# Turning the weights ahead of the codes, and 24 of 128 one-hot columns on ScalarE, in a product-key expert stage

## The reference

```
x_norm = x * rsqrt(mean(x * x) + eps) * norm_w
q = (x_norm @ wq).reshape(B, T, HEADS, 2, DIM_KEY)              # 8 heads, 2 halves, 32
sim = einsum('bthpd,hkpd->pbthk', q, keys)                      # 64 keys for each half
s1, i1 = top_k(sim[0], 16);  s2, i2 = top_k(sim[1], 16)
all_idx = (i1[..., :, None] * 64 + i2[..., None, :]).reshape(B, T, HEADS, 256)
all_scores = (s1[..., :, None] + s2[..., None, :]).reshape(B, T, HEADS, 256)
final_scores, pk = top_k(all_scores, 16)
final_idx = take_along_axis(all_idx, pk)
hidden = einsum('btd,bthkd->bthk', x_norm, expert_down[final_idx])
hidden = gelu(hidden) * relu(final_scores)
out = einsum('bthk,bthkd->btd', hidden, expert_up[final_idx])
```

## Time and profile before

| | us |
|---|---|
| median of 3 runs | 2354.24 |
| the runs | 2340.14 to 2354.62 |
| the profiled execution | 2347.7 |
| its span, first to last instruction | 2346.0 |
| first and last start of L2000 (expert stage's one-hots) | 648.1 and 1781.7 |

### The profile page before, as it was taken

The page is one execution under the profiler, slowest core; times in us unless marked ns, Lnnn a source line. Parts: engine busy times, 40 slices in busy tenths (PEclk is TensorE's granted clock), DMA queues, the critical chain, the costliest instruction groups (busy, mean ns, idle before and its releaser), DMA issues. The chain is left out here.

```text
span 2346.0 us, 48081 instructions
## 1 busy us (share of the span) xinstructions
PE 1891.4 (81%) x17539; PEld 1539.1 (66%) x17539; DVE 1628.3 (69%) x6887; ACT 732.5 (31%) x1593; POOL 558.1 (24%) x779
## 2 busy tenths in 40 slices
PE   6595899996178978889789789897889699737995
PEld 3364688874167867778677677786778577634653
DVE  3433566654999999999999999999993577420112
ACT  1343255554132231322313223132131255422220
POOL 2002344431021403304124042140431310031111
PEclk8697899998589989989899898898989799858997
DMA  2232444423500000000000000000000333212424
GB/s 61 67 103 58 103 107 102 106 49 89 131 2 6 6 2 5 2 6 6 2 6 6 2 6 2 6 6 2 2 2 1 73 83 84 87 50 78 149 99 124
DMA packets 90418, 110.21 MB, mean 47 GB/s; under 512 B 27168, under 2 KB 79088, under 8 KB 89552
## 3 DMA queue, kind: packets, MB, share of 16 engines
q1 hardware_dynamic: 84672, 99.09, 16.1%
q0 software_dynamic: 3344, 6.53, 0.8%
q10 hardware_dynamic: 2176, 1.61, 0.2%
HBM read 69.84 MB, written 33.83 MB: 44 GB/s over the span
## 5 line engine op out<-in xcount | busy, mean ns | idle before, releaser
L1568 POOL TENSOR_TENSOR peer_g<-peer_g,peer_qt 128x512 f32<-128x512 f32 (+1 forms) x208 | 250.1, 1213 | 871.1 <-ACT peer_qt L1775 871.1
L1662 PE MATMUL peer_out_ps<-peer_g,peer_up 128*128 128x256 f32 (+1 forms) x1664 | 375.5, 389 | 0.0
L1630 PE MATMUL peer_x_ps<-peer_xc,peer_dt 128*128 128x256 f32 (+1 forms) x1664 | 359.9, 379 | 0.0
L1662 PEld LDWEIGHTS peer_out_ps<-peer_g,peer_up 128*128 128x128 f32 x1664 | 324.3, 202 | 46.6
L1630 PEld LDWEIGHTS peer_x_ps<-peer_xc,peer_dt 128*128 128x128 f32 x1664 | 313.3, 195 | 42.0
L1284 DVE TENSOR_REDUCE l_attn_mx<-l_attn_s_ps 98x4 f32<-98x392 f32 (+1 forms) x320 | 174.7, 559 | 142.2 <-PE l_attn_s_ps L1054 102.5
L1652 PE MATMUL peer_x_ps<-peer_oh_h,peer_oh_a 128*128 128x32 bf16 x3136 | 167.8, 180 | 86.3 <-DVE peer_oh_l L2004 85.7
L1652 PEld LDWEIGHTS peer_x_ps<-peer_oh_h,peer_oh_a 128*128 128x128 bf16 x3136 | 163.1, 99 | 102.2 <-issue 59.0
L2000 DVE TENSOR_TENSOR peer_oh_a<-peer_a_t,peer_iota_f 128x8192 bf16<-128x8192 bf16 x49 | 216.5, 4419 | 1.3
L1775 ACT ACTIVATE peer_qt<-peer_x_ps 128x512 f32<-128x512 f32 (+1 forms) x208 | 119.1, 573 | 239.3 <-PE peer_x_ps L1630 223.5
L1205 ACT ACTIVATE l_attn_pt<-l_attn_st_ps 98x392 f32<-98x392 f32 x320 | 148.3, 492 | 142.4 <-PE l_attn_st_ps L1067 141.3
(11 more groups left out here) (325 smaller groups left out, 3536.7 us busy)
## 6 DMA issues: line engine op xcount, KB each, us to landing
moe_w<-in_L_ffn_w_dram SPq DMA_DIRECT2D x16, 1024.0 KB, 7.8
l_attn_pieces_q_dram<-l_attn_pieces_q SPq DMA_DIRECT2D x16, 294.0 KB, 3.9
l_attn_pieces_k_dram<-l_attn_pieces_k SPq DMA_DIRECT2D x16, 294.0 KB, 3.1
l_attn_stq<-l_attn_pieces_q_dram SPq DMA_DIRECT2D x16, 294.0 KB
l_attn_stk<-l_attn_pieces_k_dram SPq DMA_DIRECT2D x16, 294.0 KB
peer_g<-n_L_ffn_expert_down_dram SPq DMA_DIRECT2D x8, 512.0 KB
peer_up<-in_L_ffn_expert_up_dram SPq DMA_DIRECT2D x2, 2048.0 KB, 17.8
moe_expert_in<-l_blank SPq DMA_DIRECT2D x16, 197.5 KB
```

The source lines that it names most:

```text
L1568: nc.gpsimd.tensor_tensor(pair, pair, act_out[jp % 2][:, :, 0:cols], ALU.mult).then_inc(g_done, 1)
L1630: mm = nc.tensor.matmul(x_ps[b][:, jj * CT:jj * CT + cols], dt[:, k, 2 * jp + jj, :], xc[p][:, k, 0:cols], start=(k == 0), stop=(k == KC - 1))
L1662: mm = nc.tensor.matmul(out_ps[:, m * CT:m * CT + cols], up[:, j, m * P:(m + 1) * P], g[:, j, 0:cols], start=(j == 0), stop=(j == J - 1))
```

## The change

Five things change, all in `peer_ffn`.

The weights no longer go with the codes. When the second top-16 is through, VectorE sets a semaphore (`found`); ScalarE clamps the weights and splits off the high part (`split_weights`), GpSimd subtracts for the low part (`low_parts`), TensorE turns both after the first half of `experts_out` (`turn_weights`), and ScalarE copies them to `wh_t` and `wl_t` (`weights_out`). `low_weights` on VectorE goes.

The column code is made before the row code, and each has its own signal. TensorE turns the columns of both tiles into `tr_ps` and then the rows of both into `sim_ps[1]`; ScalarE copies them in the order b, a, b, a.

VectorE's row one-hots cover columns 0 to 103. ScalarE makes columns 104 to 127 (`side_columns`): for each of the 24 columns it writes the absolute difference of `a_t` and the column's number, 64 tokens, and then one pass over all 24 writes relu(1 - difference).

The column one-hots (`oh_l`) now come first in `one_hots`, and `add_out` stands behind the third block in place of the first.

`side_columns` for blocks 0 and 1 stands at the head of ScalarE's chunk; for block hb + 2 it stands behind the copies of block hb.

The core of the diff:

```diff
-        codes = behind(1, 3 * PP, 3 * PP, F32).rearrange("t (s k) -> t s k", s=3)
+        codes = behind(1, 3 * PP, 2 * PP, F32).rearrange("t (s k) -> t s k", s=2)
+        w_all, w_high, w_low = (behind(1, (5 + i) * PP, PP, F32) for i in range(3))
+        w_rounded = behind(1, 7 * PP, PP // 2, BF16)
...
-        TURN_AT = J // 2
+        WEIGHTS_AT, TURN_AT = (0, J - 1), (1, J // 2 - 1)
...
+            nc.gpsimd.iota(col_bias[:, 0:ACOLS], [[-1, ACOLS]], base=ACOLS - P, channel_multiplier=0,
+                           allow_small_or_imprecise_dtypes=True).then_inc(iota_done, 1)
+            nc.gpsimd.memset(col_bias[:, ACOLS:ACOLS + 1], 1.0).then_inc(iota_done, 1)
...
+            def low_parts(n):
+
+                pool.wait_ge(w_split, n + 1)
+                nc.gpsimd.tensor_tensor(w_low, w_all, w_high, ALU.subtract).then_inc(low_made, 1)
...
                     index_steps(n + 1)
+                    low_parts(n + 1)
...
-            def turn(n, t, rows):
-                pe.wait_ge(codes_ready, n + 1)
-                wait(pe, tr_ready, NTILE * n + t)
-                wait(pe, wl_ready, NTILE * n + t)
-                for s in range(3):
-                    mm = nc.tensor.transpose(tr_ps[:, s * TT:s * TT + rows], codes[0:rows, s, t * NP:(t + 1) * NP], ident[0:rows, 0:rows])
-                mm.then_inc(tr_done, 1)
+            def turn_weights(n, tiles):
+                pe.wait_ge(low_made, n + 1)
+                pe.wait_ge(sim_ready, NTILE * n + len(tiles))
+                for s, source in enumerate((w_high, w_low)):
+                    for t, rows in enumerate(tiles):
+                        mm = nc.tensor.transpose(sim_ps[0][:, (s * NTILE + t) * TT:(s * NTILE + t) * TT + rows],
+                                                 source[0:rows, t * NP:(t + 1) * NP], ident[0:rows, 0:rows])
+                mm.then_inc(w_tr_done, 1)
+
+            def turn(n, tiles):
+                wait(pe, b_ready, NTILE * n)
+                wait(pe, sim_ready, NTILE * n + len(tiles))
+                for s, bank in ((1, tr_ps), (0, sim_ps[1])):
+                    pe.wait_ge(codes_ready, 2 * n + 2 - s)
+                    for t, rows in enumerate(tiles):
+                        nc.tensor.transpose(bank[:, t * TT:t * TT + rows], codes[0:rows, s, t * NP:(t + 1) * NP],
+                                            ident[0:rows, 0:rows]).then_inc(tr_done, 1)
...
                 pe.wait_ge(oh_ready, NHB * n + hb + 1)
+                pe.wait_ge(side_ready, NHB * n + hb + 1)
...
-                        if m == KC - 1 and j == TURN_AT:
-                            for t, rows in enumerate(next_rows):
-                                turn(n + 1, t, rows)
-                mm.then_inc(out_done, 1)
+                        if m == KC - 1 and j == J - 1:
+                            mm.then_inc(out_done, 1)
+                        if (m, j) == WEIGHTS_AT and next_rows:
+                            turn_weights(n + 1, next_rows)
+                        if (m, j) == TURN_AT and next_rows:
+                            turn(n + 1, next_rows)
...
-            def turned(n, t, rows):
-                act.wait_ge(tr_done, NTILE * n + t + 1)
-                ts = slice(t * TT, t * TT + rows)
-                if t == 0:
-                    wait(act, oh_ready, NHB * n)
-                for dst, c in ((wh_t, 2), (a_t, 0), (b_t, 1)):
-                    ins = nc.scalar.activation(dst[:, ts, :], tr_ps[:, c * TT:c * TT + rows].unsqueeze(2).broadcast_to([P, rows, R]), ACT.Copy)
-                ins.then_inc(tr_ready, 1)
-
-            for t in range(NTILE):
-                turned(0, t, TT)
+            def side_columns(n, hb):
+                q = hb % 2
+                wait(act, m_done, 16 * n + 4 * (hb - 1))
+                act.wait_ge(a_ready, NTILE * n + hb // 2 + 1)
+                ts = slice(hb * HT, (hb + 1) * HT)
+                for k in range(ACOLS):
+                    ins = nc.scalar.activation(oh_a[q][:, :, P - ACOLS + k], a_t[:, ts, 0], ACT.Abs, bias=col_bias[:, k:k + 1])
+                ins.then_inc(abs_done, 1)
+                act.wait_ge(abs_done, NHB * n + hb + 1)
+                side = oh_a[q][:, :, P - ACOLS:P]
+                nc.scalar.activation(side, side, ACT.Relu, scale=-1.0, bias=col_bias[:, ACOLS:ACOLS + 1]).then_inc(side_ready, 1)
+
+            def split_weights(n):
+                act.wait_ge(found, n + 1)
+                fv = f16.rearrange("t h k -> t (h k)")
+                nc.scalar.activation(w_rounded, fv, ACT.Relu).then_inc(rounded, 1)
+                nc.scalar.activation(w_all, fv, ACT.Relu)
+                act.wait_ge(rounded, n + 1)
+                nc.scalar.activation(w_high, w_rounded, ACT.Copy).then_inc(w_split, 1)
+
+            def weights_out(n, cols):
+                act.wait_ge(w_tr_done, n + 1)
+                wait(act, oh_ready, NHB * n)
+                for s, dst in enumerate((wh_t, wl_t)):
+                    ins = nc.scalar.activation(dst[:, 0:cols, :], sim_ps[0][:, s * CT:s * CT + cols].unsqueeze(2).broadcast_to([P, cols, R]), ACT.Copy)
+                ins.then_inc(w_ready, 1)
+
+            def turned(n, tiles):
+                for t, rows in enumerate(tiles):
+                    ts = slice(t * TT, t * TT + rows)
+                    for i, (dst, bank, ready) in enumerate(((b_t, tr_ps, b_ready), (a_t, sim_ps[1], a_ready))):
+                        act.wait_ge(tr_done, 2 * NTILE * n + (i + 1) * len(tiles))
+                        nc.scalar.activation(dst[:, ts, :], bank[:, t * TT:t * TT + rows].unsqueeze(2).broadcast_to([P, rows, R]),
+                                             ACT.Copy).then_inc(ready, 1)
+
+            split_weights(0)
+            weights_out(0, CT)
+            turned(0, [TT] * NTILE)
 
             def chunk(n, p, now, then):
                 next_rows = tile_rows(then)
+                n_hb = now // HT
+                for hb in range(min(2, n_hb)):
+                    side_columns(n, hb)
                 wait(act, out_done, n)
-                for hb in range(now // HT):
+                for hb in range(n_hb):
                     scattered(n, hb)
                     if hb == 0 and then > 0:
                         wait(act, g_done, NPAIR * n)
                         query_out(n + 1, then)
                     if 0 < hb <= len(next_rows):
                         score_out(n + 1, hb - 1, next_rows[hb - 1])
+                    if hb + 2 < n_hb:
+                        side_columns(n, hb + 2)
                 hidden_out(n, now)
-                for t, rows in enumerate(next_rows):
-                    turned(n + 1, t, rows)
+                if then > 0:
+                    split_weights(n + 1)
+                    weights_out(n + 1, then)
+                turned(n + 1, next_rows)
...
-                chain.step(nc.vector.tensor_scalar(codes[:, 2, :], fv, 0.0, None, ALU.max))
+                nc.vector.memset(pad[:, 7:8], 0.0).then_inc(found, 1)
+                wait(dve, tr_done, 2 * NTILE * n)
...
-                nc.vector.tensor_tensor(row, by_rank(t1), by_rank(i1), ALU.add)
                 nc.vector.scalar_tensor_tensor(column, by_rank(t1), -0.5, by_rank(i2), ALU.mult, ALU.add).then_inc(codes_ready, 1)
-
-            def low_weights(n, t, rows):
-                dve.wait_ge(tr_ready, NTILE * n + t + 1)
-                ts = slice(t * TT, t * TT + rows)
-                nc.vector.tensor_tensor(wl_t[:, ts, :], tr_ps[:, 2 * TT:2 * TT + rows].unsqueeze(2).broadcast_to([P, rows, R]),
-                                        wh_t[:, ts, :], ALU.subtract).then_inc(wl_ready, 1)
+                nc.vector.tensor_tensor(row, by_rank(t1), by_rank(i1), ALU.add).then_inc(codes_ready, 1)
...
-                nc.vector.tensor_tensor(view(oh_a[q]), spread(a_t, P), number(P), ALU.is_equal)
-                chain.step(nc.vector.tensor_tensor(view(oh_l[q]), spread(b_t, J), number(J), ALU.is_equal))
+                def view(m, columns):
+                    return m[:, :, 0:columns].rearrange("p t (r s) -> p t r s", s=R)
+                if hb % 2 == 0:
+                    dve.wait_ge(b_ready, NTILE * n + hb // 2 + 1)
+                chain.step(nc.vector.tensor_tensor(view(oh_l[q], J), spread(b_t, J), number(J), ALU.is_equal))
+                if hb % 2 == 0:
+                    dve.wait_ge(a_ready, NTILE * n + hb // 2 + 1)
+                nc.vector.tensor_tensor(view(oh_a[q], P - ACOLS), spread(a_t, P - ACOLS), number(P - ACOLS), ALU.is_equal)
+                dve.wait_ge(w_ready, n + 1)
                 chain.wait()
-                nc.vector.tensor_tensor(view(oh_h[q]), view(oh_l[q]), spread(wh_t, J), ALU.mult)
-                nc.vector.tensor_tensor(view(oh_l[q]), view(oh_l[q]), spread(wl_t, J), ALU.mult).then_inc(oh_ready, 1)
+                nc.vector.tensor_tensor(view(oh_h[q], J), view(oh_l[q], J), spread(wh_t, J), ALU.mult)
```

(13 more changed lines are left out.)

22 lines of the change are left out of this document (12 added, 10 removed).

## The result

The changed kernel takes 2377.0 us (median of four runs, 2370.6 to 2378.3) where the kernel before takes 2352.5 (four runs beside it, 2340.1 to 2354.6): ratio 1.011, 95% interval 1.007 to 1.015. The forecast was 2358 and no change, within 2294 to 2411. The time lies in the range, 19 us over the forecast, and the change is a small loss instead of none. The profiled execution has a span of 2374.8 us beside 2346.0 before, 28.8 us more. That is 24.1 of the 28.8.

What follows compares the result with a forecast made beforehand. VectorE was taken as the limit, TensorE with 4.2 us in hand. VectorE 7.9 us quicker nearly cancels against `hidden` 3.4 later and 1.0 of clock: chunk 95.8 for 95.5, twelve steps +4 us, median 2358, range 2294 to 2411.

Steps and rivals of the forecast that it cites:

- The two rounds: Expert stage, per chunk: VectorE's round alone gives 87.6 us; the round through ScalarE and TensorE gives 63.8 + 4S.
- `hidden` at 12.5 + 4S: `hidden` starts 12.5 + 4S us after TensorE begins to turn the codes, forecast 44.5 in place of 41.1.
- S: ScalarE's time for one block of side columns: 23p + the last narrow pass + the Relu, forecast 8.0 us.
- p: Time from one narrow ScalarE pass to the next in a block of side columns: taken as 0.27 us, bounds 0.21 to 0.306.
- After `hidden`: TensorE from the start of `hidden` to the next turn: `hidden` 28.8, `experts_out` 20.8, weights' transposes 0.7, together 50.3 us.
- The lower clock: More of `hidden` may run at TensorE's lower clock as pauses between scatters grow: 1 us a chunk, bounds 0 and 2.
- The edges: First and last chunk of the stage were said to follow the same rules as the others and given no term.
- the two rivals counted there: Strided writes costing in full (chance 0.30) and the narrower view losing VectorE's rate (0.05): together 0.35 for slower by over 1%.
- strided writes: Rival at the 96 narrow passes per chunk: strided writes cost in full, kernel 2399, to 2411 with the clock; chance 0.30.
- the dear bound: Narrow passes with the full surcharge for strided writes: p = 0.306, S = 8.85, chunk 99.2 us, +45 us.
- the passes are cheaper than their nearest row: Rival: narrow passes below the nearest row's 0.257 us; at p = 0.21 the kernel takes 2292; chance 0.25.
- The narrower view: Rival at VectorE's row one-hots: 104 of 128 columns run at half speed, chunk 101.8 us, kernel 2430; chance 0.05.

Runs made afterwards that it cites:

- after: The changed kernel with 24 side columns on ScalarE and the weights turned ahead, against the kernel before: 2377.0 us, ratio 1.011.
- before: The kernel without the change, VectorE making all 128 columns and codes and weights turned together: 2352.5 us, median of four runs.

## Why the prediction was near, and where it was off

**The two rounds.** Right, and shown. VectorE's round was put at 87.6 us with 24 columns; it never sets the pace there, but the 88.5 of an undisturbed step with 16 columns, less eight columns at 0.13, is 87.4. The weights' part of it (7.9 less 4 x 0.83) was 4.6 us a chunk, and without columns the chunk fell by 4.1, or by 4.6 in an undisturbed step (90.9).

**`hidden` at 12.5 + 4S.** Right: with the S measured, 8.68, that is 47.2, and it starts at 46.9.

**S.** This is the term that was mis-sized. It was 8.0 and is 8.68, 2.7 us a chunk. Of the three parts the Relu was right (1.56 forecast, 1.57 measured). p was 0.27 and is 0.276 in the mean, 0.14 us over 23 passes. The last narrow pass, put at 0.35, lasts 0.81, and the Relu waits for its end. The sentence that "64 writes that end 0.05 later mostly fall into the overlap of 0.1" is where it failed. The first pass of a block alone ends 0.24 later than a dense one (0.60 for 0.36). For six passes that delays nothing, the next starts 0.244 later as with dense writes, while each lasts 0.04 longer than the one ahead (0.60 to 0.81); from there on the passes come 0.285 apart. The reading that fits is a queue of writes that fills by the 0.04 of each pass and is then full; the runs show the times, not the queue.

**After `hidden`.** Put at 50.3 us, and 1 us more for the clock; it is 49.2 (46.87 to 96.07). The lower clock that was feared in `hidden` did not come: 0.99 there where it was 0.96 before, and the longer pauses between scatters only lowered the stretch ahead of it (0.79 for 0.83), which ScalarE sets. So a middle chunk that does not start late comes to 96.1, and the forecast of 95.8 was near because two errors of over 2 us cancel, which is luck.

**The edges, given no term.** These make the rest of the miss. The steps of after stand against those of before as +3.9 and +2.2 for the first two, +6.5 for the last, some +2.7 for each of three chunks in the middle in which ScalarE starts late, and +0.6 for the other six: 24 us. The last step is the plainest. The last chunk has 64 tokens, so its codes are ready sooner, and before that step took 89.0 us since TensorE waited for nothing at its turn; after it takes 95.5, like any other, since TensorE's own round cannot be shortened by fewer codes. "Follow the same rules" was wrong exactly because the limit moved from one engine to the other. The first two steps are the same case. Before, VectorE had no output to add in the first chunk (0.7 us, and the 1.5 of waiting ahead of it, fall away) and waited only 0.31 in the second, so these steps took 92.9 and 94.0; after, ScalarE's chain does not get shorter by that, and they take 96.8 and 96.2. That leaves about 1 us of the first step open. Of the late starts the written-out loop shows that they are the loop's; without them the three chunks fall by 5.2 us and the rest rise by 2.2, and why the rest rise is open.

**Signs named ahead.** ScalarE gapless, TensorE not waiting, passes 0.276 apart (within 0.245 to 0.287), a block on VectorE of 7.0 (6.95): seen. `hidden` at 44 to 45 is not, it starts at 46.9. VectorE's idle time was put at 8 us ahead of the one-hots; it is 9.2, but 2.58 there, 1.10 at the scatter, 3.55 at the scores and 2.01 at GpSimd's sums. That matters: the first tile's scores stand behind the third block on ScalarE (their copies end 34.3 us after the turn), and the sums behind most of `hidden`. So VectorE hangs on ScalarE's chain too: its codes come only 1.5 us before they are asked for, and any more for ScalarE would delay both.

**The range and the chances.** The upper end follows from the sum; the lower, 2294, does not: 2354 - 62 is 2292, and 2280 with no clock term. The most likely class was "within 1%", at 0.40. At 1.1% the result lies just past it, in "slower by over 1%" (0.35), but not as the two rivals counted there had it. VectorE kept its rate. Of strided writes p stayed under the 0.287 from which they were to decide, while with the longer last pass S came out as p = 0.299 would have made it ((8.68 - 1.8)/23); that was offset by 2.1 us behind `hidden`, and most of the 24 us lie in the edges and the late starts.

**The rivals.** Strided writes did not cost in full, but in part, and this is shown by dense and stepped writes with the reads alike: 0.244 and 0.285 apart, where the dear bound was 0.306 and decided from 0.287 on. What was said against it, that the write side is idle more than half of the time, did not hold: 64 such writes take 0.285 us, more than the 0.244 from one dense pass to the next. The page of the Trainium skill that was cited, SBUF — State Buffer, section Specifications (TRN2), says that such accesses cost. For the writes the trace agrees, with 0.04 us a pass from one start to the next; reads 8 bytes apart, two to a line, cost 5 ns a pass at most. That the passes are cheaper than their nearest row holds for dense writes alone (0.244 for 0.257). The narrower view keeps VectorE's rate: 3618 ns for 104 columns beside 4416 for 128 is 0.819, where 104/128 is 0.8125.

## What to carry to other kernels

Work shared between two engines has an optimum, and the price on either side is to be set against the other: a column saved VectorE 0.13 us a chunk and cost ScalarE, and with it TensorE's start, 1.35. So the share is chosen by where the two rounds meet (16 columns here, of the counts that were run), not by how idle the second engine looks. And where a change moves the limit to another engine, steps that were short for the first engine's reasons, at the stage's start and end, have to be worked out anew.

## What the runs showed of the hardware

ScalarE's writes of 2 bytes at steps of 256 bytes go at 64 in 0.285 us, 4.5 ns each, while the passes themselves could start every 0.244. For the first six passes of a block they delay nothing: the passes start 0.244 apart while their durations grow from 0.60 to 0.81 us. From there on the passes start 0.285 apart. Blocks of 8, 16 and 24 passes show the same. Reading a tile across, elements 128 bytes apart, cost ScalarE 0.49 us for 512 elements, 0.96 ns each, with writes of eight columns in a row in both cases.
